# Three attentions: only the parts of the maxima are turned, and transfers put them under the queries

## The reference

```
scores = jnp.einsum('bqhd,bkhd->bhqk', q, k) / jnp.sqrt(jnp.float32(D))
scores = jnp.where(causal, scores, jnp.float32(-1e+30))      # in the causal one alone
p = jax.nn.softmax(scores, axis=-1)
y = jnp.einsum('bhqk,bkhd->bqhd', p, v).reshape(B, T, C) @ proj_w
```

## Time and profile before

| | |
|---|---|
| median of 3 runs | 1628.59 us (1627.82 to 1650.92) |
| the profiled execution, its own time | 1630.4 us |
| its span, first to last instruction | 1628.7 us |
| PE busy | 1406.0 us, 86% of the span |
| DVE, ACT, POOL busy | 987.6, 687.7, 628.2 us |
| mean granted clock of PE | 0.916 |

### The profile page before, as it was taken

How to read it: one execution, slowest core, us unless ns; L and a number is a source line. 1 busy time by engine, 2 the same in 40 slices (tenths; PEclk the granted TensorE clock), 3 DMA queues, 4 the chain that set the end, 5 groups by cost and what they waited for, 6 DMA issues and landing times. The chain is left out here.

```text
span 1628.7 us, 23696 instructions
## 1 busy us (share of the span) xinstructions
PE 1406.0 (86%) x9145; PEld 715.1 (44%) x9145; DVE 987.6 (61%) x1770; ACT 687.7 (42%) x1204; POOL 628.2 (39%) x626
## 2 busy tenths in 40 slices
PE   7868786988989999899868999899999877889984
PEld 3345443433334444444334444454445433355542
DVE  4898939777742211468566773745556344588866
ACT  2444432766742000257534774244434432355522
POOL 2487734354223221333124312533421312356762
PEclk8889997989999999879987998999999978999996
DMA  5000010000020000100001002000000010000000
GB/s 111 0 1 0 1 48 1 1 1 1 1 82 1 1 0 0 53 1 1 11 0 54 2 2 47 1 2 1 2 1 2 2 31 1 7 1 2 2 1 28
DMA packets 17382, 20.65 MB, mean 13 GB/s; under 512 B 7835, under 2 KB 13195, under 8 KB 16760
## 3 DMA queue, kind: packets, MB, share of 16 engines
q1 hardware_dynamic: 15440, 17.33, 3.6%
q10 hardware_dynamic: 1832, 1.80, 0.5%
HBM read 17.94 MB, written 1.05 MB: 12 GB/s over the span
## 5 line engine op out<-in xcount | busy, mean ns | idle before, releaser
L1852 DVE CUSTOM_DVE_ANT_0 P<-P,L2f_mask 128x128 f32<-128x128 f32 (+3 forms) x256 | 118.5, 521 | 99.9 <-PE P L1744 99.9
L1029 DVE TENSOR_REDUCE L0f_nm<-P 128x2 f32<-128x768 f32 (+3 forms) x88 | 97.5, 1120 | 38.1 <-PE P L926 37.9
L2028 PE MATMUL P<-L0m_hm,L0m_w 128*128 128x512 f32 x256 | 112.2, 597 | 0.0
L1822 ACT ACTIVATE L2f_prob<-P 128x1024 f32<-128x1024 f32 x80 | 80.6, 1025 | 73.1 <-PE P L1756 73.1
L1663 POOL TENSOR_SCALAR_AFFINE_SELECT L2f_prob<-L2f_prob 128x512 f32<-128x512 f32 x64 | 39.9, 638 | 161.4 <-ACT L2f_prob L1822 161.4
L983 ACT ACTIVATE L0f_prob<-P 128x512 f32<-128x512 f32 x160 | 86.9, 610 | 33.8 <-PE P L937 32.5
L1744 PE MATMUL P<-L2f_ks,L2f_qs 48*128 48x512 f32 (+3 forms) x512 | 90.9, 467 | 0.3 <-DVE L2f_nm L1852 0.3
L1756 PE MATMUL P<-L2f_qs,L2f_ks 49*128 49x256 f32 (+3 forms) x512 | 84.5, 444 | 3.1 <-DVE L2f_nm L1852 2.3
L2431 POOL TENSOR_TENSOR L3x_exm<-L3x_exm,L3x_rec 128x2048 f32<-128x2048 f32 x16 | 72.4, 4530 | 24.1 <-DVE L3x_rec L2617 24.1
L1306 PE MATMUL P<-ident,L0x_pv 128*128 128x128 f32 x384 | 53.7, 305 | 27.1 <-POOL L0x_pv L1207 27.1
L880 POOL TENSOR_SCALAR_AFFINE_SELECT L0f_prob<-L0f_prob 128x512 f32<-128x512 f32 x64 | 39.9, 638 | 95.2 <-ACT L0f_prob L983 88.3
(11 more groups left out here) (578 smaller groups left out, 3329.5 us busy)
## 6 DMA issues: line engine op xcount, KB each, us to landing
L0m_w<-in_L0m_w SPq DMA_DIRECT2D x1, 2048.0 KB, 8.0
L0f_va<-in_L0f_va SPq DMA_DIRECT2D x3, 512.0 KB, 5.3
L0x_prod<-in_x SPq DMA_DIRECT2D x2, 512.0 KB, 5.9
L0x_segi<-in_segb SPq DMA_DIRECT2D x1, 1024.0 KB, 18.2
L0m_w<-in_L0m_w SPq DMA_DIRECT2D x1, 1024.0 KB, 10.0
out<-out_o SPq DMA_DIRECT2D x4, 256.0 KB, 2.4
L1x_va<-in_va SPq DMA_DIRECT2D x3, 256.0 KB, 3.1
L1x_vr<-in_vr SPq DMA_DIRECT2D x3, 256.0 KB, 4.1
```

Of the source, the lines that this page charges most:

```text
L1029: nc.vector.tensor_reduce(S.nm[:, qt, first:first + 2 * many].rearrange("p (i e) -> p e i", e=2), P[:, bank:bank + 2, 0:many * width].rear ...
L1822: nc.scalar.activation(S.prob_of(b, g)[:, at:at + 2, :], P[:, bank:bank + 2, :], ACT.Exp).then_inc(*S.act_done.up())
L1852: m = nc.vector.tensor_tensor_reduce(out=at, in0=at, in1=mask[:, T - width:T], scale=1.0, scalar=-3.0e38, op0=ALU.add, op1=ALU.max, accum_ ...
L2028: m = mm(P[:, slot(b, i) + part, :], w1[:, e, part * 512 + i * 128:part * 512 + i * 128 + 128], hm[b % 2][:, e, :], start=e == 0, stop=e = ...
```

## The change

In the three stages the parts of the maxima no longer go into the queries' columns. `split_max` writes them into a small tile `nx` of 24 columns for each of the four query tiles: for the even and the odd head of a pair, three parts, four pairs. A step t2 (`turn_max`; one for each half, named w) turns this tile alone: 4 transposes of 128 x 24. ACT copies 24 x 512 elements to `mt` (`copy_max`), and two transfers on SP's queue (`move_max`), one for the even and one for the odd heads, put its 12 rows of 1 KB each under the queries in `qs1`, in 3 partitions. The units read `qs1` and wait for both transfers (`wait_max`); `qs2` is gone.

The orders are changed with it. In the cross stages t2 moves from the head of its half, behind two rounds of the next one, to the end of the half before it, behind U7 and ahead of the output projection. In the causal stage t2 moves from behind R0 to behind x1 and ahead of C1, the last round R10 moves from behind x1 to ahead of B5, and the step max from the end of the list to behind B5, ahead of tv and x1. The very first t2 of a stage comes right behind its step max. The rewriting of `qx` and `qk` for the sequence after the next waits for t1, no longer for t2.

The core of the diff; the causal class gets the same tiles, SP loop and copy as the cross class:

```diff
         self.vstep, self.pstep = c("vstep"), c("pstep")
         sb = ph.sb
         self.qx = [sb(f"qx{i}", [128, QT, H, 64], BF16) for i in range(2)]
         self.qs1 = [sb(f"qs1{i}", [128, 8, T], BF16) for i in range(2)]
-        self.qs2 = [sb(f"qs2{i}", [128, 4, T], BF16) for i in range(2)]
         self.ks = [sb(f"ks{i}", [128, 8, keys], BF16) for i in range(2)]
         self.xq, self.xqr = sb("xq", [128, QT * H, 8]), sb("xqr", [128, QT * H, 8])
         self.nm, self.nmr = sb("nm", [128, QT, H]), sb("nmr", [128, QT, 8])
+        self.nx, self.mt = ([sb(f"{n}{i}", shape, BF16) for i in range(2)] for n, shape in (("nx", [128, QT, 2, 3, 4]), ("mt", [24, T])))
         self.ot, self.rec = sb("ot", [128, 4, QT * 4, 32]), sb("rec", [128, 4, QT * 4])
         self.on, self.ont = sb("on", [128, QT * 4, 4, 8]), sb("ont", [128, T])
         self.wo = sb("wo", [128, C])
...
@@ -389,13 +390,44 @@
     def split_max(self, dve, b, half):
 
         nc = self.nc
-        at = self.qslots(b)[:, :, 8 * half:8 * half + 8, :]
-        nm, nmr = self.nm[:, :, 8 * half:8 * half + 8].unsqueeze(3), self.nmr[:].unsqueeze(3)
-        part = [at[:, :, :, 48 + p:49 + p] for p in range(3)]
+        if b:
+            dve.wait_ge(self.ring_full.sem, self.place["t2", b - 1, half])
+        nm, nmr = (a.rearrange("p t (i e) -> p t e i", e=2) for a in (self.nm[:, :, 8 * half:8 * half + 8], self.nmr[:]))
+        part = [self.nx[half][:, :, :, p, :] for p in range(3)]
         link(dve, nc.vector.tensor_copy(part[0], nm), self.vstep)
         link(dve, nc.vector.tensor_tensor(nmr, nm, part[0], ALU.subtract), self.vstep)
         link(dve, nc.vector.tensor_copy(part[1], nmr), self.vstep)
         nc.vector.tensor_tensor(part[2], nmr, part[1], ALU.subtract).then_inc(*self.nx_ready.up())
+
+    def turn_max(self, pe, step):
+
+        _, b, half = step
+        pe.wait_ge(self.nx_ready.sem, 2 * b + half + 1)
+        bank = self.ring_use(pe, step)
+        out = self.P[0:24, bank, :].bitcast(BF16)
+        for qt in range(QT):
+            m = self.nc.tensor.transpose(out[:, qt * 128:(qt + 1) * 128],
+                                         self.nx[half][:, qt].rearrange("p e x i -> p (e x i)"), self.G["identb"][:])
+        m.then_inc(*self.ring_full.up())
+
+    def copy_max(self, act, step):
+
+        _, b, half = step
+        bank = self.ring_view(act, step)
+        if b:
+            act.wait_ge(self.rows_ready.sem, 32 * (2 * (b - 1) + half + 1))
+        self.nc.scalar.copy(self.mt[half][:], self.P[0:24, bank, :].bitcast(BF16)[:, 0:T]).then_inc(*self.act_done.up())
+
+    def move_max(self, sp, step):
+
+        _, b, half = step
+        sp.wait_ge(self.act_done.sem, max(self.freed[step], self.freed["t1", b, 2 * half], self.freed["t1", b, 2 * half + 1]))
+        for e in range(2):
+            sp.dma_start(self.qs1[b % 2][64 * e + 48:64 * e + 51, 4 * half:4 * half + 4, :],
+                         self.mt[half][12 * e:12 * e + 12, :]).then_inc(*self.rows_ready.up(16))
+
+    def wait_max(self, pe, b, half):
+        pe.wait_ge(self.rows_ready.sem, 32 * (2 * b + half + 1))
...
-STEP = """t0 R0 R1 w0 w1 l0 R2 U1 U0 R7 l2 l1 S0 U2 rec R3 t1 U3 R4 U4 m0 U6 R5 turn S1 R6 max tk U5 res m1 U7 out m2 xq q""".split()
+STEP = """t0 R0 R1 l0 R2 U1 U0 R7 l2 l1 S0 U2 rec R3 t1 U3 R4 U4 m0 U6 R5 turn S1 R6 max tk U5 res m1 U7 w out m2 xq q""".split()
...
+        if kind == "w":
+            return ("t2", (h + 1) // 2, (h + 1) % 2) if more else None
...
-    order += spread_between(lead, rounds(0)) + [("max", 0, 0)]
+    order += spread_between(lead, rounds(0)) + [("max", 0, 0), ("t2", 0, 0)]
...
             load_all(sp, ld_tables, tables)
+            for s in S.order:
+                if s[0] == "t2":
+                    S.move_max(sp, s)
...
                 elif kind == "t2":
-                    pe.wait_ge(S.nx_ready.sem, 2 * b + n // 2 + 1)
-                    S.turn_q(pe, s)
+                    S.turn_max(pe, s)
...
                 elif kind == "unit":
                     bank, e, half = S.ring_use(pe, s), n % 2, n // 8
-                    pe.wait_ge(S.act_done.sem, S.freed["t2", b, n // 4])
-                    mm(P[:, bank, :], S.ks[b % 2][64 * e:64 * e + 51, n // 2, 0:128], S.qs2[half][64 * e:64 * e + 51, n // 2 % 4, :],
+                    S.wait_max(pe, b, half)
+                    mm(P[:, bank, :], S.ks[b % 2][64 * e:64 * e + 51, n // 2, 0:128], S.qs1[b % 2][64 * e:64 * e + 51, n // 2, :],
                        start=True, stop=True).then_inc(*S.ring_full.up())
...
+                if kind == "t2":
+                    S.copy_max(act, s)
+                    continue
...
-STEP_causal_order = """sa0 R0 w0 w1 R1 la A0 B0 t0 k0 R2 B2 A1 lb A2 R5 A4 C0 k1 R4 A6 lc lt rec sb0 sc0 B6 R3 B4 A3 R7 A7 ma C2 B3 R6 t1 turn R8 p0 A5 mb x0 R9 B1 sa1 mc p1 sb1 B5 mt B7 x1 R10 conv C1 out C3 sc1 max res""".split()
+STEP_causal_order = """sa0 R0 R1 la A0 B0 t0 k0 R2 B2 A1 lb A2 R5 A4 C0 k1 R4 A6 lc lt rec sb0 sc0 B6 R3 B4 A3 R7 A7 ma C2 B3 R6 t1 turn R8 p0 A5 mb x0 R9 B1 sa1 mc p1 R10 sb1 B5 max mt B7 x1 w C1 conv out C3 sc1 res""".split()
...
-                    pe.wait_ge(S.act_done.sem, max(S.freed["t2", b, h // 4] for h, *_ in tiles))
+                    S.wait_max(pe, b, half)
                     for h, kt, at, q0, width in tiles:
                         e, pair = h % 2, h // 2
                         m = mm(P[:, bank, at:at + width], S.ks[b % 2][64 * e:64 * e + 51, pair, kt * 128:(kt + 1) * 128],
-                               S.qs2[half][64 * e:64 * e + 51, pair % 4, q0:q0 + width], start=True, stop=True)
+                               S.qs1[b % 2][64 * e:64 * e + 51, pair, q0:q0 + width], start=True, stop=True)
```

More of the change, by code:

```diff
@@ L370, in split_q @@
         if b > 1:
-            pool.wait_ge(self.ring_full.sem, max(self.place["t2", b - 2, i] for i in range(4)))
+            pool.wait_ge(self.ring_full.sem, max(self.place["t1", b - 2, i] for i in range(4)))
         at = self.qx[b % 2][:].rearrange("p t h c -> p (t h) c")
@@ L466, in one @@
             return (kind if half == 0 else {"q": "kv", "xq": "xkv"}[kind], b + 2, 0) if b + 2 < NB else None
-        return {"w": ("t2", b, 2 * half + n), "U": ("unit", b, 8 * half + n), "S": ("rest", b, (half, n))}[kind]
+        return {"U": ("unit", b, 8 * half + n), "S": ("rest", b, (half, n))}[kind]
     order = [("kv", 0, 0), ("z", 0, 0), ("q", 0, 0), ("xkv", 0, 0), ("xq", 0, 0), ("z", 1, 0), ("z", 2, 0), ("z", 3, 0),
@@ L638, in _ @@
                                    P[:, bank, :].bitcast(BF16)[:, 0:4 * PAD]).then_inc(*S.act_done.up())
-                elif kind == "t2":
-                    nc.scalar.copy(S.qs2[n // 2][:, 2 * (n % 2):2 * (n % 2) + 2, :].rearrange("p i t -> p (i t)"),
-                                   P[:, bank, :].bitcast(BF16)).then_inc(*S.act_done.up())
                 else:
```

22 lines of the change are left out of this document (13 added, 9 removed).

## The result

The changed kernel takes **1694.1 us** (median of 4 runs, 1688.37 to 1705.01); the kernel before took 1632.9 in the runs beside it. The ratio is **1.036** (95% interval 1.031 to 1.042): slower by over 2%, far above the forecast of 1637 and outside its range. The profiled execution took 1694.98 us with a span of 1693.2, against 1630.4 and 1628.7 before.

What follows compares the result with a forecast made beforehand. PE, working in written order, was taken to set the pace. Causal +3.6 and both cross stages +3.6 summed to +7 us, giving 1637; eight-in-ten range 1606 to 1655, this case's own 1630 to 1650.

Steps and rivals of the forecast that it cites:

- The steps of a turn: Passage between half-batches, 8 a stage, the first the lead: last scores, maximum, split, t2, then units, A0 first.
- the ring's order: Causal turns 1 to 4: t2 takes p1's PSUM bank, so waits for value transpose and x1, 1.7 us more.
- The losses at the lead and the last two turns of the cross stages: Each cross stage: first unit later by 1.5 us in the lead, 1.5 at the seventh turn, 1.2 at the last.
- the price of the clock: Causal turns 1 to 4: at 1.2 GHz A0 comes 2.5 us later each, +10 if all four lose the clock.
- so I take half of the turns: Causal turns 1 to 4: only half lose the clock, putting the stage at +3.6 us.
- +0.2 each: Causal turns 5 to 7, without p1: first unit at 430.5 against 430.32, computed on turn 6.
- +3.6: Causal stage: -1.4 us at full clock, +8.6 with all four turns slowed, +3.6 with half of them.
- the upper sum: Causal stage: +8.6 us, if turns 1 to 4 all lose the clock, by the advice against idle gaps.
- the chain of 3.55 us: From t2 to first unit: four transposes 0.27, hand-over 0.2, copy to unit 3.10; ends last at most causal turns.
- The gain lands: Rival, three stages: PE's busy share is the bound, 19.3 us saved come through, 1609 to 1611; chance 0.27.
- the doubt about PE's busy share: Cross stage: weight loads take 51.6 of 113 us, so PE has room and saved work is worth under 19 us.
- The transfer is dear: Rival, all 24 turns: landing takes 3.9 us instead of 1.9, each turn 2 us later, near 1685; chance 0.07.

Runs made afterwards that it cites:

- e1: The kernel before with the new order alone, still 16 transposes, two copies and no transfers a turn: 1676.8 us, ratio 1.027.
- e11: The kernel before with the new order, x1 ahead of the split and useless matmuls ahead of each causal t2: 1662.4 us, ratio 1.016.
- e8: The changed kernel with useless matmuls in the cross stages only, at the lead and the last two turns: 1673.1 us, ratio 1.021.
- e2: The changed kernel without its 48 transfers, units waiting for the copy alone, maxima left out and exponents scaled: 1663.7 us, ratio 1.019.
- e5: The changed kernel's 4 transposes, copy and transfers in the order of the kernel before: 1744.4 us, ratio 1.066.
- e9: The changed kernel with causal work moved around t2, x1 ahead of the split, and useless matmuls in causal and cross stages: 1644.6 us, ratio 1.006.
- e10: The kernel before with useless matmuls sized to each idle time ahead of causal t2, more in the cross leads: 1627.6 us, ratio 0.994.
- e7: The kernel before with 5 useless matmuls (14 in the lead) ahead of the split's wait at each causal t2: 1631.1 us, ratio 0.998.
- e4: The changed kernel with x1 ahead of the split and 8 useless matmuls (14 in the lead) ahead of each causal t2: 1683.0 us, ratio 1.029.

## Why the prediction was wrong, step by step

**Right.** The steps of a turn. In turns 1 to 4 t2 is released by x1's last copy, as the ring's order said. In turn 2 t2 starts 4.48 us after the start of the reduction (332.21 to 336.69); the prediction's 324.64 to 329.1 is 4.46. At the low clock t2 to A0 was to take 6.0 us; it takes 5.8. The losses at the lead and the last two turns of the cross stages have the right place and sign, though at the last turn it is the value transpose, not the transfer, that PE waits for.

**Wrong: the price of the clock, and that alone moves the result out of the range.** The prediction's step was: "At that pace the 3.4 us of work take 6.0 and A0 comes 2.5 us later than written above: all four turns, +10". It stopped at A0. I had one row of a low level over 4.8 us and took that as the length everywhere; here the level stays at 0.50 for 10 to 27 us from turn 1 on, through a good part of the half. The trace of the kernel before had a longer one that the prediction did not use, in the lead of its first cross stage:

```profile
699.60:719.90 20.30, 18.66 (x113) 9.32 (x110) 11.50 (x20) 10.05 (x16) 2.74 (x6) 0.50 0.00 1
```

The next step, "so I take half of the turns", failed too: it was all four, and also turns 5 to 7, whose idle time of 2.35 us (1.79 at turn 6 before) I had put down at +0.2 each. Where +3.6 stood for the causal stage, 42.9 was measured, and e1 shows that the order makes most of it (30.7). That it does so largely by idle time that turns into low clock is what e11 speaks for, with the reservation made there. The Trainium skill (TensorE: Matmul & The Clock Gate, Why this matters for your kernels), whose advice against idle gaps the prediction weighed as the upper sum, agrees with the trace at the lead and turns 1 to 4, where idle times of 3.97 to 7.52 us were followed by the low level. At turns 5 to 7 it followed 2.35 us too, less than the gaps that the page warns of; there the measurement decides. The mistake was to price what it advises against by the turn and not by the half. The prediction also let the chain of 3.55 us end last at most causal turns; a transfer released a causal unit just once, since PE's own work up to A0, at the low level, took longer.

**Wrong in the same way: the waits of the cross stages.** +1.5 for the seventh turn and +1.2 for the last were booked as waits. The interval from 7th to 8th split grew by 3.3 and 5.1 us, the tail by 7.9 and 3.0. e8 took 14 us out without shortening the wait for the transfer. There the wait was uncovered, and the work behind it ran at half rate.

**Mis-sized: the transfer and the transposes.** The chain from copy to unit was 3.6 to 4.0 us, not 3.10; each transfer carries 12 KB where the latent stage's carries 8. The rule that I cited from the Trainium skill (DMA: Bandwidth & Descriptors, Why small descriptors are slow), that transfers within SBUF don't suffer from small pieces, isn't decided by this, since rows and bytes both differ. The 12 transposes are worth 0.5 us a turn where nothing else ends later, not 0.8, and in the middle turns of the cross stages the order takes as much.

**The rivals.** "The gain lands" is out: in the middle turns PE's busy time fell by 1.2 us of 50 and the turns got no shorter. But what was saved did come through: against e1, which has the same order, busy time and turns fell by the same 2.0 us, and it is the order that takes them back. So the doubt about PE's busy share that the prediction took from the Trainium skill (Perfetto Trace Analysis, Identifying the Most-Contended Engine) is not what decided here. "The transfer is dear" came near the total, with 1685, by luck, since its mechanism is wrong: it put the decision at a landing 1 us or more longer than the latent stage's, and the chain was only some 0.5 to 0.9 longer. The transfers do cost 30 us (e2), 25 of them in the cross stages, through the uncovered waits and the clock, and some 108 in an order that doesn't cover them (e5: 1744 against 1636 beside it).

**Open.** Why the low level lasts 24 us behind t2 at turn 2 here with PE busy in all of 345 to 360, 11 with the same causal code in e8, and was left within some 5 us before, after a longer idle time, no run shows. Of the causal stage's 43 us I can't say what share, if any, the transfers hold: the order alone gave 31, and two executions of the same causal code differed by 11. Whether the change can be made to gain at all in the causal stage was not tried beyond e9.

## What to carry to other kernels

When a change adds idle time to PE, look at the granted clock behind each idle time of the profile, and price the whole stretch that runs at the lower level, with the longest such stretch as the upper end, not only the work up to the next wait. Before shortening PE's work, ask what covers the latency that the new way brings: 12 transposes were worth 0.5 us, the transfer in their place needs 3.6 us of other work behind it, and the order that provides it cost more than was saved. Where idle time can't be removed, matmuls without a use, sized to it and written into a bank that is waiting anyway, gave back 14 us in two stages (e8) and 0.6% of a kernel in which nothing else was changed (e10); where they were too few, or the next wait took over, they gave back nothing that could be measured (e7, e4).

## What the runs showed of the hardware

Filling idle time shortened stages in which PE was already busy for most of the time: in e8 both cross stages together went from 285.2 to 271.1 us with more work on PE and the wait for the transfer as long as before, at a granted clock of 0.92 instead of 0.85. Idle times of 2.35 us in front of t2 were followed by windows at 0.50 in three of three turns of the changed kernel, but with the same code in e8 in two of three; 1.26 and 1.79 before were not the earlier trace rows. A transfer of two times 12 KB within SBUF, issued by SP, released its unit 3.5 to 4.0 us after the start of the copy that feeds it. And the same causal code took 281.6 and 270.6 us in two executions: with a clock that falls for stretches of changing length, a stage's length is not one number.
